# Which engine masks the attention probabilities: the products on TensorE replaced by GpSimd, 16 graphs of 512 nodes

## The reference

```python
h = jnp.maximum(_layernorm(x, axis=-1), 0.0)          # x: (16, 512, 512) float32
q = heads(h @ Wq + bq); k = heads(h @ Wk + bk); v = heads(h @ Wv + bv)   # 16 heads of 32
scores = jnp.einsum('bhqd,bhkd->bhqk', q, k) * scale
scores = jnp.where(adj[:, None] == 0, -jnp.inf, scores)
attn = jax.nn.softmax(scores, axis=-1)
out = jnp.einsum('bhqk,bhkd->bhqd', attn, v)
return x + (out.transpose(0, 2, 1, 3).reshape(b, s, D_MODEL) @ Wo + bo)
```

## Time and profile before

| | |
|---|---|
| median of 3 runs | 1709.16 us (1708.68 to 1709.55) |
| the profiled execution | 1711.46 us |
| its span, first to last instruction | 1709.7 us |
| busy: PE, DVE, ACT, POOL | 1655.3, 1527.0, 1477.9, 153.1 us |
| granted TensorE clock, mean | 0.990 of full speed |

### The profile page before, as it was taken

How to read it: one execution, slowest core, us unless ns; L and a number is a source line. 1 busy time by engine, 2 the same in 40 slices (tenths; PEclk the granted TensorE clock), 3 DMA queues, 4 the chain that set the end, 5 groups by cost and what they waited for, 6 DMA issues and landing times.

```text
span 1709.7 us, 27479 instructions
## 1 busy us (share of the span) xinstructions
PE 1655.3 (97%) x7876; PEld 1035.4 (61%) x8001; DVE 1527.0 (89%) x3656; ACT 1477.9 (86%) x3498; POOL 153.1 (9%) x203
## 2 busy tenths in 40 slices
PE   6899999999999999999999999999999999999997
PEld 5556666666666666666665666666666666666653
DVE  4799998989989899998999989899998999989895
ACT  3799898898888989899898988989899888989985
POOL 2001100001010011100011000111100001000001
PEclk9799999999999999999999999999999999999998
DMA  6433343333433334343333433344343433433320
GB/s 198 107 86 100 106 111 90 113 90 110 116 95 108 88 113 109 100 108 89 114 92 109 114 92 106 93 118 111 102 106 86 112 96 106 114 97 94 92 85 26
DMA packets 117166, 175.18 MB, mean 102 GB/s; under 512 B 30860, under 2 KB 32920, under 8 KB 117016
## 3 DMA queue, kind: packets, MB, share of 16 engines
q1 hardware_dynamic: 112536, 171.83, 37.3%
q10 hardware_dynamic: 4480, 1.58, 0.4%
HBM read 54.79 MB, written 16.78 MB: 42 GB/s over the span
## 4 chain that ended last, share of the span: by engine, by line
PE 78%; DVE 15%; issue 3%; ACT 2%; SPq 1%; DMA 0%; DVEq 0%; ACTq 0%
PE ps L797 14%; PE psO L831 13%; PE psP L700 13%; PE psP L701 11%; PE ps L811 11%; PE psP L702 11%; DVE ps L592 5%; DVE probs L599 4%; PE ps L814 2%; PE ps L747 1%; DVE x_tile L513 1%; DVE stats L505 1%; ACT ps L430 1%; DVE y_tile L626 1%; DVE oT_lo L613 1%
## 5 line engine op out<-in xcount | busy, mean ns | idle before, releaser
L592 DVE CUSTOM_DVE_ANT_0 ps<-ps,bias_q 128x512 f32<-128x512 f32 x1024 | 708.7, 694 | 132.5 <-PE ps L797 122.4
L430 ACT ACTIVATE ps<-ps,neg_max 128x512 f32<-128x512 f32 x1024 | 686.9, 671 | 92.1 <-DVE neg_max L592 75.6
L470 ACT ACTIVATE probs<-ps 128x512 f32<-128x512 f32 x1024 | 622.5, 608 | 72.0 <-PE ps L814 37.7
L599 DVE SCALAR_TENSOR_TENSOR probs<-bias_k,probs 128x512 f32<-128x512 bf16 x768 | 552.9, 721 | 8.2 <-ACT probs L470 8.1
L797 PE MATMUL ps<-k_stack,q_stack 96*128 96x512 f32 x1024 | 450.8, 441 | 21.3 <-ACT ps L430 11.5
L811 PE MATMUL ps<-q_stack,k_stack 98*128 98x512 f32 x1024 | 410.0, 401 | 3.2 <-ACT probs L470 3.0
L797 PEld LDWEIGHTS ps<-k_stack,q_stack 96*128 96x128 f32 x1024 | 193.6, 189 | 277.0 <-ACT ps L430 132.2
L831 PE MATMUL psO<-probs,v_sb 128*32 128x512 f32 x2048 | 274.5, 608 | 2.0 <-DVE oT_lo L613 0.9
L811 PEld LDWEIGHTS ps<-q_stack,k_stack 98*128 98x128 f32 x1024 | 194.9, 190 | 40.1 <-ACT probs L470 14.9
L430 ACT ACTIVATION_READ_ACCUMULATOR ps<-ps,neg_max 128x1 f32 x1024 | 218.2, 213 | 0.0
L592 DVE DVE_READ_ACCUMULATOR2_ANT neg_max<- 128x1 f32 x1024 | 144.0, 141 | 0.0
(11 more groups left out here) (75 smaller groups left out, 1882.2 us busy)
## 6 DMA issues: line engine op xcount, KB each, us to landing
q_stack<-part_hi SPq DMA_DIRECT2D x512, 64.0 KB, 2.0
k_stack<-part_hi SPq DMA_DIRECT2D x504, 64.0 KB, 2.0
x_tile<-in_x_dram SPq DMA_DIRECT2D x64, 256.0 KB, 2.9
y_tile<-in_x_dram SPq DMA_DIRECT2D x64, 256.0 KB, 2.9
adj_tile<-in_adj_dram SPq DMA_DIRECT2D x64, 256.0 KB, 3.0
q_stack<-part_lo SPq DMA_DIRECT2D x256, 64.0 KB, 2.0
k_stack<-part_lo SPq DMA_DIRECT2D x256, 64.0 KB, 2.0
out_dram<-y_tile SPq DMA_DIRECT2D x62, 256.0 KB, 2.1
```

The lines of the kernel that those rows point to most:

```text
L430: nc.scalar.activation(item, item, ACT.Exp, scale=-1.0, bias=neg_max[:, g % 2, col:col + 1], accum_out=exp_sum[:, col:col + 1]).then_inc(e ...
L470: nc.scalar.activation(probs[:, n % P_RING, :], ps2[:, n % 2, :], ACT.Exp, scale=SCALE).then_inc(exp2_done, 1)
L592: nc.vector.tensor_tensor_reduce(bank1(("s", u)), bank1(("s", u)), bias_q[:, qt, :], -SCALE, 3.0e38, ALU.add, ALU.min, neg_max[:, g % 2, c ...
L599: nc.vector.scalar_tensor_tensor(out=probs[:, n % P_RING, :], in0=bias_k[:, n % 16 // 4, :], scalar=-MASKED, in1=probs[:, n % P_RING, :], ...
```

## The change

- The list VECTOR_MASKED is replaced by ON_GPSIMD = (4, 5, 6, 12, 13, 14, 15), for n % 16: GpSimd masks heads 0 to 2 of key tile 1 and all heads of key tile 3. VectorE masks the other 9 of 16. TensorE's product L814 is gone.
- GpSimd masks by an integer product of the probabilities' bits with keep_k, 0 or 1 in int32. keep_k holds the odd key tiles, bias_k only the even ones. VectorE's one tile of key tile 1 reads keep_k too.
- ScalarE fills the two by two activations of 512 columns instead of one of 1,024. The second "m" turn moves from slot 61 to slot 62.
- GpSimd's order is now written by slots: masks, form_rstd and the sums with bo.
- The first output tile waits for one group of heads at each quarter instead of for all four at its first.
- The product with V waits for both engines' masks. The wait for bias_k moves from TensorE to the masking engines.

```diff
-VECTOR_MASKED = (0, 1, 2, 4, 5, 6)
+ON_GPSIMD = (4, 5, 6, 12, 13, 14, 15)
-         24: [("c", 2, -1)], 40: [("c", 3, -1)], 53: [("m", 0, 0)], 56: [("c", 0, 0)], 61: [("m", 1, 0)]}
+         24: [("c", 2, -1)], 40: [("c", 3, -1)], 53: [("m", 0, 0)], 56: [("c", 0, 0)], 62: [("m", 1, 0)]}
...
-        bias_k = sb("bias_k", [P, NT, S], BF16)
+        bias_k = sb("bias_k", [P, NT // 2, S], BF16)
+        keep_k = sb("keep_k", [P, NT // 2, S], I32)
...
+            def mask(b, n):
+                kt = n % 16 // 4
+                if n < 16 and n % 4 == 0:
+                    pool.wait_ge(m_done, due(2 * b + kt // 2 + 1))
+                pool.wait_ge(exp2_done, due(64 * b + n + 1))
+                bits = probs[:, n % P_RING, :].bitcast(I32)
+                nc.gpsimd.tensor_tensor(bits, bits, keep_k[:, kt // 2, :], ALU.mult).then_inc(gpsimd_masked, 1)
+
             def step(k, parity):
-                if k > 0:
-                    form_rstd(k, 2)
-                    if k - 2 != LAST:
-                        add_bo(k - 2, 2)
-                    form_rstd(k, 3)
-                    if k - 2 != LAST:
-                        add_bo(k - 2, 3)
-                for t in range(2):
-                    form_rstd(k + 1, t)
-                for t in range(NT if k - 1 == LAST else 2):
-                    add_bo(k - 1, t)
+                for u in range(SLOTS):
+                    b, n = pass2(k, u)
+                    if have(b) and n % 16 in ON_GPSIMD:
+                        mask(b, n)
+                    if k > 0 and u == 5: form_rstd(k, 2)
+                    if u == 8 and k - 2 != LAST: add_bo(k - 2, 2)
+                    if k > 0 and u == 9: form_rstd(k, 3)
+                    if u == 12 and k - 2 != LAST: add_bo(k - 2, 3)
+                    if u in (41, 43): form_rstd(k + 1, (u - 41) // 2)
+                    if u == 47: add_bo(k - 1, 0)
+                    if u == 54: add_bo(k - 1, 1)
+                    if u in (54, 55) and k - 1 == LAST: add_bo(LAST, u - 52)
...
-                            act.wait_ge(scores2, due(64 * (k - 1) + 48 + 8 * n + 8))
-                            act.wait_ge(probs_masked, due(MASKED_ALL * (k - 1) + masked_before(48 + 8 * n + 8)))
-                            nc.scalar.activation(bias_k[:, 2 * n:2 * n + 2, :], bank1((kind, n, rel)).bitcast(BF16).rearrange("p (t q) -> p t q", q=S),
-                                                 ACT.Identity).then_inc(m_done, 1)
+                            turned = bank1((kind, n, rel)).bitcast(BF16)
+                            act.wait_ge(vector_masked, due(vector_before(64 * (k - 1) + 48 + 8 * n + 8)))
+                            nc.scalar.activation(bias_k[:, n, :], turned[:, 0:S], ACT.Identity).then_inc(bias_k_done, 1)
+                            act.wait_ge(gpsimd_masked, due(gpsimd_before(64 * (k - 1) + 48 + 8 * n + 8)))
+                            nc.scalar.activation(keep_k[:, n, :], turned[:, S:2 * S], ACT.Identity,
+                                                 scale=-1.0 / MASKED, bias=1.0).then_inc(m_done, 1)
...
-                    if have(b) and n % 8 in VECTOR_MASKED:
+                    if have(b) and n % 16 not in ON_GPSIMD:
+                        kt = n % 16 // 4
...
+                        tile = probs[:, n % P_RING, :]
+                        if kt % 2 == 0:
+                            nc.vector.scalar_tensor_tensor(out=tile, in0=bias_k[:, kt // 2, :], scalar=-MASKED, in1=tile,
+                                                           op0=ALU.add, op1=ALU.min).then_inc(vector_masked, 1)
+                        else:
+                            nc.vector.scalar_tensor_tensor(out=tile, in0=keep_k[:, kt // 2, :], scalar=-MASKED, in1=tile,
+                                                           op0=ALU.mult, op1=ALU.min).then_inc(vector_masked, 1)
...
-                    if T == 0:
-                        pe.wait_ge(o_hi_done, due(4 * b + 4))
-                        pe.wait_ge(o_lo_done, due(4 * b + 4))
...
+                if T == 0 and kind == "o":
+                    pe.wait_ge(o_hi_done, due(4 * b + kt + 1))
+                    pe.wait_ge(o_lo_done, due(4 * b + kt + 1))
...
-                        if g == 0 and j == 0:
-                            pe.wait_ge(m_done, due(2 * b + kt // 2 + 1))
                         pe.wait_ge(exp2_done, due(64 * b + n - 1))
-                        last = nc.tensor.matmul(ps2[:, n % 2, :], k_stack[:, g, j, P * kt:P * kt + P], q_stack[:, g, j, :],
-                                                start=True, stop=(n % 8 in VECTOR_MASKED))
-                        if n % 8 not in VECTOR_MASKED:
-                            last = nc.tensor.matmul(ps2[:, n % 2, :], ident_b[:], bias_k[:, kt, :], start=False, stop=True)
-                        last.then_inc(scores2, 1)
+                        nc.tensor.matmul(ps2[:, n % 2, :], k_stack[:, g, j, P * kt:P * kt + P], q_stack[:, g, j, :],
+                                         start=True, stop=True).then_inc(scores2, 1)
```

More of the change, by code:

```diff
@@ L138, in attention_block @@
         bias_done = sem("bias_done")
-        m_turned, m_done = sem("m_turned"), sem("m_done")
+        m_turned, bias_k_done, m_done = sem("m_turned"), sem("bias_k_done"), sem("m_done")
         qkv_done, out_done = sem("qkv_done"), sem("out_done")
@@ L146, in attention_block @@
         scores2, exp2_done = sem("scores2"), sem("exp2_done")
-        probs_masked = sem("probs_masked")
+        vector_masked, gpsimd_masked = sem("vector_masked"), sem("gpsimd_masked")
         pv_done, o_hi_done, o_lo_done = sem("pv_done"), sem("o_hi_done"), sem("o_lo_done")
@@ L196, in pass2, with gpsimd_before, vector_before @@
             return (k, u - S2_AT) if u >= S2_AT else (k - 1, u + SLOTS - S2_AT)
-        def masked_before(n):
-            return n // 8 * len(VECTOR_MASKED) + sum(i < n % 8 for i in VECTOR_MASKED)
-        MASKED_ALL = masked_before(SLOTS)
+        def gpsimd_before(n):
+            return n // 16 * len(ON_GPSIMD) + sum(i < n % 16 for i in ON_GPSIMD)
+        def vector_before(n):
+            return n - gpsimd_before(n)
         def load_stack(queue, b, i, pieces=("hi0", "lo", "hi1")):
@@ L595, in step @@
                     b, n = pass2(k, u - 1) if u else pass2(k - 1, SLOTS - 1)
-                    if have(b) and n % 8 in VECTOR_MASKED:
-                        dve.wait_ge(exp2_done, due(64 * b + n + 1))
-                        nc.vector.scalar_tensor_tensor(out=probs[:, n % P_RING, :], in0=bias_k[:, n % 16 // 4, :], scalar=-MASKED,
-                                                       in1=probs[:, n % P_RING, :], op0=ALU.add, op1=ALU.min
-                                                       ).then_inc(probs_masked, 1)
+                    if have(b) and n % 16 not in ON_GPSIMD:
+                        kt = n % 16 // 4
+                        if n < 16 and kt % 2 == 0:
+                            dve.wait_ge(bias_k_done, due(2 * b + kt // 2 + 1))
+                        elif n < 16:
+                            dve.wait_ge(m_done, due(2 * b + kt // 2 + 1))
+                        dve.wait_ge(exp2_done, due(64 * b + n + 1))
+                        tile = probs[:, n % P_RING, :]
[5 more added lines that the diff above has]
+                                                           op0=ALU.mult, op1=ALU.min).then_inc(vector_masked, 1)
                     if u in C_AT:
@@ L827, in step @@
                         pe.wait_ge(exp2_done, due(64 * b + 4 * n + 4))
-                        pe.wait_ge(probs_masked, due(MASKED_ALL * b + masked_before(4 * n + 4)))
+                        pe.wait_ge(vector_masked, due(vector_before(64 * b + 4 * n + 4)))
+                        pe.wait_ge(gpsimd_masked, due(gpsimd_before(64 * b + 4 * n + 4)))
                         for j in range(GROUP):
```

## The result

| | before | after |
|---|---|---|
| median of 5 runs each, same chip | 1709.55 us | 1699.71 us |
| ratio after / before | | 0.9937 (95%: 0.9924 to 0.9949) |
| span of the profiled execution | 1709.7 us | 1697.7 us |

The change gained 0.6%, some 11 us, where 40.5 had been forecast. The time of 1699.7 us lies inside the range of 1648 to 1702, but the gain is a quarter of the forecast, and the range reached that far only for rival (b), whose mechanism did not come true: that is luck.

What follows compares the result with a forecast made beforehand. In the steady part the time was taken to be TensorE's count of matmuls. Terms -54.5 - 2 + 3 + 5 + 2 + 2 + 4 = -40.5 us, from the median 1709.16, gave 1668.7 us; range 1648 to 1702.

Steps and rivals of the forecast that it cites:

- rival (b): ScalarE becomes the bound in part; half the gain turns into waits for exponentials: 1682 to 1700 us, chance 0.18.
- Part 1: TensorE without its 256 mask products: 234 of them counted at 0.233 us, -54.5 us (from -60 to -48).
- Part 2: 448 masks on GpSimd, 576 instead of 768 on VectorE; a batch's first slots: -2 us (from -15 to +18).
- The chain behind the load of y: GpSimd's sum with bo waits for its load, masks queue behind it in a batch's first slots: +0.5 us a batch.
- The meetings: GpSimd and VectorE masks sharing access to SBUF, 9 places a batch, mean 0.02 us: +3 us (0 to +45).
- Part 3: Batch's first slots: output tile's wait and later mask turn together; wait on ScalarE replaces VectorE's: +5 us (-11 to +9).
- Part 4: The rest: slot 53 copies +2 us, ScalarE's steady slots +2, and the tail (last 20 us) +4 (-1 to +8).
- The last run: Last four tiles, all GpSimd's, 5.2 us of masks: last product with V +2.3 us, sums ahead add 0.5.
- (a): All that TensorE gives up comes back, and the old oT_lo wait too: -58 us, 1651 us, chance 0.16.
- the old wait: TensorE's 0.53 us at a batch's first slot for the last oT_lo, 9.3 us over the run; forecast to go.
- (d): Slower: GpSimd's integer product takes over 2 us; with 2.6 us a mask, 168 us more, 1837 us; chance 0.15.
- (c): Every one of the 9 GpSimd-VectorE meetings in a batch falls out badly for VectorE: 1711 us, no change; chance 0.05.

## Why the prediction was wrong

**Part 1, -54.5 us: failed by its size.** The price of a product, 0.233 us, is right where TensorE is busy throughout: four steady slots went from 6.11 to 5.89. Over all of slots 16 to 59 a product gave 0.18 us without any other edit and 0.20 in the changed kernel; where the rest went is open. The step that failed is the count of those on the path. I took out 16 and 6, and left in all the others, those of slots 2 to 15 among them, although the same text says that VectorE is on the path in a batch's first 16 slots. Measured alone, all 256 gave 37 us, and those in a batch's first 16 slots gave none of it. This is the largest miss, 17 us.

**Part 2, -2 us for the first slots: wrong in sign.** I booked VectorE's 12 masks less in a batch as a relief of 0.65 us where it binds. But the change moves them: in slots 4 to 8 VectorE has tiles 7 to 11, five masks, where it had three. Slots 4 to 7 are 6.86 - 6.36 = 0.50 us a batch longer than in the kernel without mask products, and leaving VectorE's mask of tile 7 out takes that back (6.34). Slots 8 to 11 are 7.43 - 6.91 = 0.52 longer, which is not the number of masks but the meeting (next paragraph). Slots 12 to 15 give 0.42 us back. The chain behind the load of y was named, with 0.5 us a batch; moving the sum gave 0.57. It was looked for in the product with V, and came by the layer norm, which I had in the sum of GpSimd's times but followed no further.

**The meetings, +3 us: failed.** The step that failed is "mostly VectorE is first there". VectorE's masks take more than 1 us at four places in a batch of the changed kernel: 1.55 us for tile 11's in all of the 14 batches, and 1.1 to 1.3 near slots 13, 46 and 52 in nearly all. At tile 11, where VectorE is behind, the meeting costs 0.50 us: with GpSimd's mask of tile 12 held back, slots 8 to 11 (6.95) are as in the kernel without mask products (6.91). That is 7 us over the run; my highest price for a meeting was 0.33, read where VectorE had slack. What the three others cost was not measured alone.

**Part 3, +5 us: right in mechanism and near in size.** In the kernel before the pair costs 7 us (5 to 9). In the changed one slots 60 to 1 are 10.54 us where those of before without the products are 10.07. But the sum of the pair hid that the quarters are worth 11 us and the late turn takes some 19.

**Part 4, the end, +4 us: too small.** The end is 9 us longer than before. The +4 stood beside the kernel without the products, whose end is 83.9 us: against it, it is 13.2. The last run was named, the hold on VectorE's masks of tiles 56 to 59 and the lower clock were not.

**The rivals.** (a) is out, since the products give 37 us and not 59.6, and ScalarE's queue keeps what the old wait frees. (d) is out, as the integer product takes 1.31 us. (b), ScalarE as the bound in part, holds at slots 0 and 1 alone; in four steady slots TensorE does not wait for it (busy 5.89 of 5.89 us). Its band of 1682 to 1700 us holds the measured time all the same. Of (c)'s nine places four show a slowed mask, and one is shown to cost time. I had written that a few long masks in a batch speak for the forecast and eight for (c): there were four, and one was enough for more than the +3.

In all, on the profiled spans: 36 us from the products (1709.7 to 1673.7), then against that kernel +6.6 in slots 60 to 1 (0.47 x 14), +8.4 in slots 4 to 15 (0.60 x 14), -3.6 in slots 16 to 59 (0.26 x 14), +13.2 at the end and -0.9 before the first whole batch: 1673.7 + 23.7 = 1697.4, where 1697.7 was measured. For what was lost in a batch's slots 60 to 11 the experiments show the cause; of the 13.2 us at the end they show 6.6, and the rest is open.

## What to carry to other kernels

Price removed work on the bound engine only in the stretches where it binds, and where several engines take turns write the sum stretch by stretch; the same number of instructions, moved by a few slots, can be a relief on paper and a load in place. When a change bundles edits, measure each alone: here one small wait taken by pieces was worth as much as the whole, and another edit ate it. An engine that is mostly idle needs its queue read too: what matters is what stands behind its waits for a DMA, and who is late when it takes a shared port.

## What the runs showed of the hardware

GpSimd's product of two int32 tiles of 128x512 takes 1.29 us undisturbed, as long as its fp32 sum of such tiles (1.28), and VectorE masks from an int32 tile as fast as from a bf16 one (0.69 us, the median of 512 masks from bf16 and of 64 from int32). I had expected neither to be certain. Where VectorE and GpSimd meet on SBUF, adding a wait of GpSimd for VectorE made the kernel 8 us faster by the ratios (0.9727 to 0.9681): GpSimd's start 0.28 us ahead had cost VectorE 0.87 us there.
